# An LSTM recurrence with its state on both row halves, one tanh for all gates and one signal for all products of a step

## What is computed

```python
xi = xt @ U_i + b_i
xg = xt @ U_c + b_c
xo = xt @ U_o + b_o
def step(carry, xs):
    h, c = carry
    i_t = sigmoid(xi_t + h @ V_i)
    g_t = tanh(xg_t + h @ V_c)
    o_t = sigmoid(xo_t + h @ V_o)
    c_new = h * c + i_t * g_t
    h_new = o_t * tanh(c_new)
    return ((h_new, c_new), h_new)
```

## Time and profile before

| what | value |
|---|---|
| median of 3 runs | 825.37 us |
| lowest, highest | 825.3 us, 841.33 us |
| span of the profiled execution | 836.2 us |
| own time of the profiled execution | not given apart; of the three times only 841.33 lies above its span |
| mean granted clock of TensorE | 0.807 |
| PE busy | 734.4 us (88%) |
| DVE busy | 339.7 us (41%) |
| ACT busy | 288.9 us (35%) |
| POOL busy | 126.4 us (15%) |
| recurrence, window | 499 to 831 us |

### The profile page before, as it was taken

The page is one execution under the profiler, slowest core; times in us unless marked ns, Lnnn a source line. Parts: engine busy times, 40 slices in busy tenths (PEclk is TensorE's granted clock), DMA queues, the critical chain, the costliest instruction groups (busy, mean ns, idle before and its releaser), DMA issues.

```text
span 836.2 us, 13956 instructions
## 1 busy us (share of the span) xinstructions
PE 734.4 (88%) x5217; PEld 396.0 (47%) x5224; DVE 339.7 (41%) x1247; ACT 288.9 (35%) x1390; POOL 126.4 (15%) x146
## 2 busy tenths in 40 slices
PE   6899999999999999998998978888888888888886
PEld 3555555656665655544333843333433333343333
DVE  4444434444434344434546053333333333333333
ACT  2322222222222222212531014444444444444443
POOL 3333333333333333410000000000000000000000
PEclk9666655565556566667999989999899999999999
DMA  7000000000000000000000000000000000000000
GB/s 259 1 1 2 2 0 0 0 0 0 0 0 0 0 0 0 0 0 1 0 1 0 1 1 1 1 1 2 1 1 1 2 1 2 2 2 1 2 1 14
DMA packets 2578, 6.30 MB, mean 8 GB/s; under 512 B 1372, under 2 KB 1953, under 8 KB 2337
## 3 DMA queue, kind: packets, MB, share of 16 engines
q1 hardware_dynamic: 2530, 5.68, 2.0%
HBM read 5.42 MB, written 0.26 MB: 7 GB/s over the span
## 4 chain that ended last, share of the span: by engine, by line
PE 60%; DVE 19%; ACT 15%; issue 6%; POOL 1%; another core or an unknown queue 0%; DVEq 0%; POOLq 0%
PE bk L311 15%; PE bk L638 10%; DVE bk L1077 6%; ACT gp L803 5%; DVE mem L1080 5%; ACT bk L804 5%; ACT bk L808 4%; PE bk L524 4%; PE bk L423 4%; PE bk L595 3%; DVE a0y L907 2%; PE bk L433 2%; PE bk L375 1%; PE bk L542 1%; DVE hv L905 1%
## 5 line engine op out<-in xcount | busy, mean ns | idle before, releaser
L654 PE MATMUL bk<-idle 128*64 128x512 bf16 x720 | 203.0, 388 | 0.0
L638 PEld LDWEIGHTS bk<-mem,lvh 65*64 65x64 f32 x1536 | 82.0, 139 | 181.8 <-DVE mem L1080 181.6
L638 PE MATMUL bk<-mem,lvh 65*64 65x4 f32 x1536 | 104.5, 208 | 59.3 <-DVE mem L1080 59.3
L311 PE MATMUL bk<-idle 128*128 128x256 bf16 x608 | 146.5, 395 | 2.2 <-POOL lrcur L258 2.2
L1077 DVE TENSOR_TENSOR_SCAN bk<-bk,gp 64x12 f32<-64x12 f32 x256 | 46.4, 181 | 146.9 <-ACT bk L804 146.9
L803 ACT ACTIVATE gp<-bk 64x8 f32<-64x8 f32 x256 | 43.8, 171 | 151.7 <-PE bk L638 151.7
L311 PEld LDWEIGHTS bk<-idle 128*128 128x128 bf16 x608 | 67.1, 129 | 42.3 <-issue 11.5
L654 PEld LDWEIGHTS bk<-idle 128*64 128x64 bf16 x720 | 61.7, 113 | 23.3 <-issue 2.0
L274 POOL TENSOR_TENSOR mem<-mem,gcur 128x1024 f32<-128x1024 f32 x16 | 30.3, 1893 | 213.1 <-DVE mem L934 212.9
L1080 DVE SCALAR_TENSOR_TENSOR mem<-og,bk 64x4 f32<-64x4 f32 x256 | 38.3, 150 | 53.7 <-ACT bk L808 53.7
L806 ACT ACTIVATE og<-bk 64x4 f32<-64x4 f32 x256 | 42.8, 167 | 6.1
(11 more groups left out here) (273 smaller groups left out, 850.3 us busy)
## 6 DMA issues: line engine op xcount, KB each, us to landing
cw<-in_cw SPq DMA_DIRECT2D x1, 3456.0 KB, 10.9
w<-in_w SPq DMA_DIRECT2D x1, 520.0 KB
w<-in_w SPq DMA_DIRECT2D x1, 512.0 KB
xs<-in_x SPq DMA_DIRECT2D x1, 256.0 KB, 2.6
out<-xs SPq DMA_DIRECT2D x1, 256.0 KB, 2.1
memw<-in_memw SPq DMA_DIRECT2D x1, 128.0 KB, 2.1
wqkv<-in_wqkv SPq DMA_DIRECT2D x1, 96.0 KB, 2.3
c1p<-in_c1p SPq DMA_DIRECT2D x1, 66.0 KB
```

Source lines behind the costliest of these rows:

```text
L311: nc.tensor.matmul(bk[:, bank, 0:256], idle[:, 0:128], idle[:, 128:128 + 256], start=True, stop=True)
L638: return nc.tensor.matmul(bk[row:row + D, 2 * (s // CH % 2) + k, c:c + B], lvh[:, g, :], hist[:, s, :], start=False, stop=True, skip_group ...
L654: nc.tensor.matmul(bk[0:D, 5, 0:FILL_N], idle[:, 0:D], idle[:, 128:128 + FILL_N], start=True, stop=True)
```

## The change

The state is held twice, on rows 0 to 63 and again on rows 64 to 127, and all operations of the step on ACT and DVE run over 128 rows.

- Products. Each of the three gates gets its own bank with both row halves: banks 3 x (chunk mod 2) plus 1 (c), 0 (i) and 2 (o). So each gate needs two recurrent products per step, one for the output rows 0 to 63 and one for 64 to 127; c and o read the upper copy of hist and the weights, i the lower copy. They are 64 by 64, where before they were 65 by 64. Six products stand where three were, and one signal, gates_igo, after the last. `inputs_part` writes 128 output rows with one product per gate, from `luh` with its columns doubled.
- ACT. One tanh reads the step's 4 columns of three banks and writes 12 elements per row into `gx`. The factor 0.5 of the sigmoids has moved into the weights (lvh, luh). The tanh of c stays.
- DVE. The scan has four elements for each image, 16 per row, with both inputs in gx, and adds first and multiplies then. The other two operations keep 4 elements per row.
- Set-up. DVE makes lvh and luh with six operations and sets ones in gx; the clearing of bank 6 has gone. lu and lv come in at twice the size. The fills write bank 7.

```diff
-            gate_at = ((0, 0), (0, D), (1, 0))
+            gate_bank = (1, 0, 2)
...
-                k, row = gate_at[g]
-                nc.tensor.matmul(bk[row:row + D, 2 * (chunk % 2) + k, 0:CH * B], lu[:, g, :], t3T[:, chunk * CH:(chunk + 1) * CH, :],
-                                 start=True, stop=False, skip_group_check=True)
+                nc.tensor.matmul(bk[:, 3 * (chunk % 2) + gate_bank[g], 0:CH * B], luh[:, g, :],
+                                 t3T[:, chunk * CH:(chunk + 1) * CH, :], start=True, stop=False, skip_group_check=True)
...
-                return nc.tensor.matmul(bk[row:row + D, 2 * (s // CH % 2) + k, c:c + B], lvh[:, g, :], hist[:, s, :],
-                                        start=False, stop=True, skip_group_check=True)
+                rows = slice(row * D, row * D + D)
+                return nc.tensor.matmul(bk[col * D:col * D + D, 3 * (s // CH % 2) + gate_bank[g], c:c + B], lvh[rows, g, :],
+                                        hist[rows, s, :], start=False, stop=True, skip_group_check=True)
...
-                recurrent(s, 0)
-                recurrent(s, 1).then_inc(sem("gates_ig"), 1)
-                recurrent(s, 2).then_inc(sem("gate_o"), 1)
+                recurrent(s, 0, 0, 0)
+                recurrent(s, 1, 1, 0)
+                recurrent(s, 0, 0, 1)
+                recurrent(s, 1, 1, 1)
+                recurrent(s, 2, 0, 0)
+                recurrent(s, 2, 0, 1).then_inc(sem("gates_igo"), 1)
...
-                act.wait_ge(sem("gates_ig"), s + 1)
-                nc.scalar.activation(gp[:, :, 0:2], wide(bk[0:D, bank, cols], 2), ACT.Tanh)
-                nc.scalar.activation(bk[0:D, 6, 1:3 * B:3], bk[D:2 * D, bank, cols], ACT.Tanh, scale=0.5).then_inc(sem("in_gate"), 1)
-                act.wait_ge(sem("gate_o"), s + 1)
-                nc.scalar.activation(og[:, :], bk[0:D, bank + 1, cols], ACT.Tanh, scale=0.5)
+                act.wait_ge(sem("gates_igo"), s + 1)
+                nc.scalar.activation(gates_out(), bk[:, bank:bank + 3, cols], ACT.Tanh).then_inc(sem("in_gate"), 1)
...
-                nc.vector.tensor_tensor_scan(c_t.rearrange(flat3), bk[0:D, 6, 0:3 * B], gp[:, :, :].rearrange(flat3),
-                                             0.0, ALU.mult, ALU.add).then_inc(sem("c_new"), 1)
+                nc.vector.tensor_tensor_scan(c_t.rearrange("p b k -> p (b k)"), gx[:, 0:4 * B], gx[:, 32:32 + 4 * B],
+                                             0.0, ALU.add, ALU.mult).then_inc(sem("c_new"), 1)
...
-            nc.vector.memset(lvh[D:D + 1, :, :], 0.0)
-            nc.vector.tensor_scalar(lvh[0:D, :, :], lv[:, :, :], 0.5, None, ALU.mult)
+            for g, part_of in enumerate((1.0, 0.5, 0.5)):
+                nc.vector.tensor_scalar(lvh[:, g, :], lv[:, g, :], 0.5 * part_of, None, ALU.mult)
+                nc.vector.tensor_scalar(luh[:, g, :], lu[:, g, :], part_of, None, ALU.mult)
+            nc.vector.memset(gx[:, 2:16:4], 1.0)
+            nc.vector.memset(gx[:, 33:48:2], 1.0).then_inc(sem("rec_set"), 1)
```

More of the change, by code:

```diff
@@ L85, in build @@
         b3 = sb("b3", [128, 1])
-        lu = sb("lu", [D + 1, 3, D])
-        lv = sb("lv", [D, 3, D])
+        lu = sb("lu", [D + 1, 3, 2 * D])
+        lv = sb("lv", [128, 3, D])
         notfirst = sb("notfirst", [128, NT * E])
@@ L200, in build, with gates_out @@
         t3T = part(0, S, B)[0:D + 1]
[L201 to L205, removed]
+        hist = part(S * B, S + 1, B)
+        lvh = sb("lvh", [128, 3, D])
+        luh = sb("luh", [D + 1, 3, 2 * D])
+        gx = sb("gx", [128, 96])
+        og = gx[:, 67:67 + 4 * B:4]
+        p0 = sb("p0", [D, B])
+        cs = bk[:, 6, 0:8 * B].rearrange("p (n b k) -> p n b k", n=2, b=B)
+        tc = bk[:, 6, 64:64 + B]
+        def gates_out():
+            first = gx[:, 1:2]
+            return bass.AP(first.tensor, first.offset, [first.ap[0], [33, 3], [4, B]])
         warm = sb("warm", [1, 2])
@@ L246, in _ @@
             nc.gpsimd.memset(sc0[:, :, :], 0.0)
-            nc.gpsimd.memset(gp[:, :, :], 0.0)
+            nc.gpsimd.memset(gx[:, :], 0.0)
             for t in (*img, *zim):
@@ L653, in _ @@
                 for _ in range(fills if s + 1 < S else 0):
-                    nc.tensor.matmul(bk[0:D, 5, 0:FILL_N], idle[:, 0:D], idle[:, 128:128 + FILL_N], start=True, stop=True)
+                    nc.tensor.matmul(bk[0:D, 7, 0:FILL_N], idle[:, 0:D], idle[:, 128:128 + FILL_N], start=True, stop=True)
             pe.wait_ge(sem("h_new"), S + 1)
@@ L797, in _ @@
             table(ACT.Tanh)
-            act.wait_ge(sem("rec_init"), 1)
+            act.wait_ge(sem("rec_set"), 1)
             for s in range(S):
                 cols = slice(s % CH * B, (s % CH + 1) * B)
-                bank = 2 * (s // CH % 2)
-                act.wait_ge(sem("gates_ig"), s + 1)
-                nc.scalar.activation(gp[:, :, 0:2], wide(bk[0:D, bank, cols], 2), ACT.Tanh)
-                nc.scalar.activation(bk[0:D, 6, 1:3 * B:3], bk[D:2 * D, bank, cols], ACT.Tanh, scale=0.5).then_inc(sem("in_gate"), 1)
-                act.wait_ge(sem("gate_o"), s + 1)
-                nc.scalar.activation(og[:, :], bk[0:D, bank + 1, cols], ACT.Tanh, scale=0.5)
+                bank = 3 * (s // CH % 2)
+                act.wait_ge(sem("gates_igo"), s + 1)
+                nc.scalar.activation(gates_out(), bk[:, bank:bank + 3, cols], ACT.Tanh).then_inc(sem("in_gate"), 1)
                 act.wait_ge(sem("c_new"), s + 1)
-                nc.scalar.activation(bk[0:D, 6, 16:16 + B], cs[:, s % 2, :, 2], ACT.Tanh, scale=0.5).then_inc(sem("tanh_c"), 1)
+                nc.scalar.activation(tc, cs[:, s % 2, :, 3], ACT.Tanh, scale=0.5).then_inc(sem("tanh_c"), 1)
         @block.vector
@@ L1067, in _ @@
                 ins.then_inc(sem("t3T"), 1)
[L1068 to L1071, removed]
+            nc.vector.memset(p0[:, :], 0.0).then_inc(sem("h_new"), 1)
             for s in range(S):
@@ L1076, in _ @@
                     dve.wait_ge(sem("hc"), s)
-                nc.vector.tensor_tensor_scan(c_t.rearrange(flat3), bk[0:D, 6, 0:3 * B], gp[:, :, :].rearrange(flat3),
-                                             0.0, ALU.mult, ALU.add).then_inc(sem("c_new"), 1)
+                nc.vector.tensor_tensor_scan(c_t.rearrange("p b k -> p (b k)"), gx[:, 0:4 * B], gx[:, 32:32 + 4 * B],
+                                             0.0, ALU.add, ALU.mult).then_inc(sem("c_new"), 1)
                 dve.wait_ge(sem("tanh_c"), s + 1)
-                nc.vector.scalar_tensor_tensor(hist[0:D, s + 1, :], og[:, :], 1.0, bk[0:D, 6, 16:16 + B],
-                                               ALU.add, ALU.mult).then_inc(sem("h_new"), 1)
+                nc.vector.scalar_tensor_tensor(hist[:, s + 1, :], og, 1.0, tc, ALU.add, ALU.mult).then_inc(sem("h_new"), 1)
                 if s + 1 < S:
                     dve.wait_ge(sem("h_new"), s + 2)
-                    nc.vector.scalar_tensor_tensor(gp[:, :, 2], hist[0:D, s + 1, :], 0.5, c_t[:, :, 2], ALU.mult,
+                    nc.vector.scalar_tensor_tensor(gx[:, 3:4 * B:4], hist[:, s + 1, :], 0.5, c_t[:, :, 3], ALU.mult,
                                                    ALU.mult).then_inc(sem("hc"), 1)
@@ L1145, in layouts @@
     o["lu"] = np.stack([np.concatenate([a["L1_ffn_U_" + g], np.asarray(a["L1_ffn_b_" + g])[None]], axis=0) for g in "cio"], axis=1)
+    o["lu"] = np.concatenate([o["lu"], o["lu"]], axis=2)
     o["lv"] = np.stack([np.asarray(a["L1_ffn_V_" + g]) for g in "cio"], axis=1)
+    o["lv"] = np.concatenate([o["lv"], o["lv"]], axis=0)
     return {k: np.ascontiguousarray(v) for k, v in o.items()}
```

7 lines of the change are left out of this document (3 added, 4 removed).

## The result

The changed kernel takes 926.08 us (median of 6 runs, 904.72 to 950.5) against 829.7 us (6 runs, 825.3 to 841.33). Executions of one kernel differ here by how long TensorE's clock is down, and the ratio of 1.0965 (95% interval 1.0881 to 1.1049) leaves out those that stand apart from the fastest. So it is 10% slower, where 821.5 us and a range of 815 to 842 were forecast. The profiled execution is the one of 950.5 us, the longest of the six, with a span of 948.7 and a mean granted clock of 0.668. The three shortest took 904.72 to 912.96 us at a mean granted clock of 0.713 to 0.733, and seven runs of the kernel before, taken beside experiment 1, had 0.811 to 0.832: the clock is down in the short ones too, only for less of the time.

What follows compares the result with a forecast made beforehand. It took the LSTM recurrence's loop of dependences, 1.29 us a step, as the bound. Steps -6.4, shapes +0.5, lower clock +1.6 and ends +0.4 gave -3.9 us, taking the median from 825.4 to 821.5 us; range 815 to 842.

Steps and rivals of the forecast that it cites:

- Activations: ACT in each recurrence step: one tanh of 0.175 us replaces 0.33 us on the chain, saving 0.155 us.
- Products: PE in each recurrence step: ACT waits for twelve product instructions, ending at 0.41 us instead of 0.29, costing +0.12 us.
- C: Slower rival: row halves of the products don't overlap, gate i's passes queue, step 1.375, 850 us; chance 0.10.
- D: Slower rival: products on the same rows queue, upper rows eight deep, +0.22 us per step, 878 us; with E 0.05.
- F: Faster rival: gate o's passes follow gate c's 0.01 apart, 0.10 us less per step, 796 us; chance 0.07.
- E: Slower rival: the activation pays 0.06 us for each further bank, +31 us, 852 us; with D 0.05.
- Scan: DVE's scan in each recurrence step: 16 elements in place of 12, 191 ns, costing +0.01 us.
- Sum per step: Recurrence step: -0.155 + 0.12 + 0.01 = -0.025 us, so 1.265 us; over 256 steps -6.4 us.
- Fills and shapes: PE's shape changes between products and fills: hidden in plain steps, 0.5 us charged for all 45 steps with inputs' products.
- rival B: Complete drains at shape changes make PE the bound in 45 steps: +8 us, 830; grows if lower clock recurs; chance 0.10.
- The lower clock: Recurrence steps at 1.2 GHz: about 1.92 us instead of 1.66, 6.8 of them, clock mean left at 0.98: +1.6 us.
- Ends: Set-up and loads free; first inputs' products load 128 columns instead of 64: +0.4 us.

Runs made afterwards that it cites:

- experiment 1: Changed kernel with each 128 by 64 fill replaced by two 64 by 64 fills side by side, both on the upper rows: 931.35 us, ratio 1.1266.
- experiment 4: Kernel before with the tanh of c computed over 128 rows in place of 64, the lower rows unused: 839.41 us, ratio 1.0161.
- experiment 9: Changed kernel with gates c and i in one tanh over two banks and gate o beside the chain again, three 128 by 64 fills: 914.63 us.
- Experiment 10: Changed kernel with four pairs of diagonal 64 by 64 fills a step, two in steps with an inputs' product: 840.59 us, ratio 1.0168.
- experiment 2: Kernel before with its recurrent products cut from 65 rows to 64 (the 65th is all zeros), fills left 128 by 64: 886.49 us.
- 7: Kernel before with its fills made 128 by 128, products of 65 rows untouched: 871.79 us, ratio 1.0511.
- experiment 8: Kernel before with 64-row recurrent products and three diagonal pairs of 64 by 64 fills: 832.49 us, ratio 1.0008.
- experiment 3: Changed kernel with four fills a step in place of three (three in steps with an inputs' product): 845.53 us, ratio 1.0255.

## Why the prediction was wrong

Step by step, as the prediction has them:

1. *Activations* (0.175, saved 0.155): 192 ns measured. Three banks cost little, but the 128 rows do. "Twice the rows cost nothing" was taken from DVE's scans for ACT and is wrong: experiment 4 shows 15 ns for the tanh of c by rows alone, and 175 + 15 = 190 is about the new activation. In experiment 9 one bank with 4 elements took 178 ns and two banks with 8 took 185, so a further bank with its 4 elements costs 7, of which 4 are the elements' by L806 and L803. The tanh of c itself costs the same 15 ns a second time, which the sum had at nothing.
2. *Products* (+0.12): ACT starts 0.44 after the first product, 0.33 before: +0.11. The four quarters run side by side, the twelve end in 0.41, as forecast. Rivals C, D and F fall with that, and so does, a second time, the rule of the Trainium skill on weight loads (TensorE: Matmul & The Clock Gate, Part 3, The mechanism) that made D: eight loads on both row halves have begun by 760.60, while the first product, which ends at 760.72, still runs. The price per bank (E) was not 0.06 us but some 0.003; most of the 17 ns over the estimate is the rows', whose 128 cost gate o's own tanh 11 ns in experiment 9 (178 against 167).
3. *Scan* (191): 200. L1088 takes 159 for 150. What of these 9 ns each is rows and what is layout was not tried.
   Sum per step: +0.019 measured (from scan to scan 1.308 at the upper level against 1.289), -0.025 forecast. That error is 0.044 x 256 = 11 us: at an undisturbed clock the change costs 0.019 x 256 = 5 us, 0.6% of the whole, where it should have gained 0.5%. Experiment 10, whose clock was nearly undisturbed, was 1.7% slower; its recurrence took 340.1 us against 331.0. Of these 9 us 5 are the steps'; the rest was not worked out.
4. *Fills and shapes*: at a change of shape the next instruction starts 0.07 to 0.08 before the end of the one ahead, as was read off, and at the upper level it is hidden in every step, those with an inputs' product too (steps of 1.308 throughout). So rival B, PE as the bound at the upper level, didn't happen in its own form.
5. *The lower clock* is the step that failed: it priced the lower level at +1.6 us, and it cost 117. The length of a lower-level step was right (1.92 forecast, 1.94 measured), but its count was kept: "PE gets no less to do, so I leave the clock as it is". The recurrence ran at 0.61 and not at 0.98, and that is 117 of the 121 us. The reasoning judged PE by the work given to it. Experiments 2 and 7 show that a change of shape between products and fills, with as many and as long fills and an unchanged step at the upper level, takes the clock from 0.98 to 0.83 and 0.81; experiment 8 takes the shape changes out again, and 0.97 is back. Rival B had named it in half a sentence (it grows if the clock falls more often) and gave it no price. The rule of the Trainium skill that a change of tiling mode drains TensorE (TensorEngine Tiling (Array Packing), Key Properties) was weighed only for time on the chain; what it cost was the clock. The amount of filling is the other half: with a fourth fill and all the changes of shape (experiment 3) the clock was at 0.97.
6. *Ends*: their 0.4 us can't be seen. The part ahead of the recurrence ended 9 us sooner in the profiled execution of the changed kernel, with a granted clock of 0.66 against 0.62 in its first 400 us.

What goes with it: how often the clock falls and how long it stays down are two things. In windows of 1 us, the recurrence of experiment 2 has nine falls and low stretches of 10 to 24 us; the changed kernel has three falls and 18 to 144 us. So what costs most in the changed kernel is that the clock is so slow to come back. Why it stays down longer than in experiment 2 was not taken apart: a lower-level step is as long in both (1.94 and 1.93), but the changed kernel has twelve product instructions for six, and one change of shape more in its steps with an inputs' product.

Where the clock falls, on the other hand, all traces agree. One fall of the changed kernel, the inputs' products of two steps and two windows:

```profile
855.58 0.43 PE L639 MATMUL bk<-mem,luh 65*128 65x64 f32 x2
856.89 0.43 PE L639 MATMUL bk<-mem,luh 65*128 65x64 f32 x2
...
856.00:857.00 1.00, 1.00 (x16) 0.51 (x16) 0.44 (x3) 0.16 (x1) 0.00 (x0) 1.00 0.00 0
857.00:858.00 1.00, 1.00 (x4) 0.37 (x4) 0.51 (x3) 0.35 (x2) 0.00 (x0) 0.63 0.00 0
```

Twelve of the fourteen profiled executions have falls within the recurrence, 60 in all as windows of 1 us show them, those of the kernel before among them. Each lies 1 to 5 us behind the start of the first inputs' product of a chunk, thus in or just behind the three steps that give up a fill for it, though such a group of three comes only once in 16 steps, some 20 us or more after the last. Of the other two, experiment 1 never rose, and experiment 3, with three fills left in these steps, stayed up from 503 us to the end. No run changed these steps alone, so whether a full number of fills there would have saved the clock stays open.

## What to carry to other kernels

Where idle products hold TensorE's clock up, they belong to what a change must keep: give them the shape of the products around them, let them use all rows, look at the steps that have the fewest of them, and read the granted clock of a stretch at the lower level as well as at the upper before a step is priced. A gap that is hidden from the chain of waits may still cost the clock. And when operations of one step are merged, leave the one that ran beside the chain where it is: two gates in one tanh gained 0.07 us a step, three lost 0.02.

## What was not expected of the hardware

- Fills of 64 by 64 in pairs on the same 64 rows left the granted clock at 0.50 for 434 us, though PE had no idle time; the same pairs on the diagonal, over all rows, gave 0.92.
- One zero row less in six small product instructions per step (65 rows to 64) made a kernel 57 us slower in the median, through the change of shape beside three fills; with fills in the products' shape nothing was lost.
- All 60 falls of the granted clock inside the recurrence came 1 to 5 us behind the start of an inputs' product that had taken the place of a fill.
- Products in four quarters of the array, each 64 by 64, run side by side in f32: twelve instructions took 0.41 us where six took 0.40.
- ACT needs 15 ns more for 128 rows than for 64 with 4 elements per row (158 against 143).
